# Writing out the counted loops of a four-stage decoder kernel on one core

## The reference, cut to what matters

```python
x = _layernorm(x + _L0_attn_ref(x, ...))           # stage a: grouped attention with rope
x = _layernorm(x + _L0_xattn_ref(x, ctx, itok, ...))  # stage a: latent cross attention
x = _layernorm(x + _L0_ffn_ref(x, ...))            # stage b: 16 experts, 4 chosen, shared expert
x = _layernorm(x + _L1_attn_ref(x, ...))           # stage c: gated delta rule, 32 value heads
x = _layernorm(x + _L1_xattn_ref(x, ctx, mask, ...))  # stage d: 8-bit cross attention
x = _layernorm(x + _L1_ffn_ref(x, ...))            # stage d: top-1 gated attention
```

```python
A  = -(einsum(k_beta, k) * decay) * strict
Tm = solve_triangular(eye - A, eye)
u, kcd = Tm @ v_beta, Tm @ (k_beta * exp(gc))
out = (q * exp(g)) @ St + (q @ k.T * decay) @ (u - kcd @ St)
```

## Time and profile before

| what | value |
|---|---|
| runs (median of 3) | 2425.04 us (2422.2 to 2428.43) |
| the profiled execution, its own time | 2429.71 us |
| its span, first to last instruction | 2428.0 us |
| PE, matmuls, share of the span | 84% |
| DVE, ACT, POOL | 60%, 36%, 6% |
| mean granted PE clock | 0.891 of full |

### The profile page before, as it was taken

How to read it: one execution, slowest core, us unless ns; L and a number is a source line. 1 busy time by engine, 2 the same in 40 slices (tenths; PEclk the granted TensorE clock), 3 DMA queues, 4 the chain that set the end, 5 groups by cost and what they waited for, 6 DMA issues and landing times. The chain is left out here.

```text
span 2428.0 us, 30948 instructions
## 1 busy us (share of the span) xinstructions
PE 2050.6 (84%) x10836; PEld 1521.5 (63%) x10850; DVE 1460.7 (60%) x3251; ACT 880.9 (36%) x1542; POOL 140.1 (6%) x130
## 2 busy tenths in 40 slices
PE   6988987998985889898998989989899883787786
PEld 4867776554553568485684856848668582465454
DVE  3557665323222576767767667676676854657666
ACT  2433433111113445443453534535345431333233
POOL 1011010000002000000000000000000001011110
PEclk8889888999996889999999999999999995787787
DMA  3000000400001120301203012030120202000000
GB/s 125 5 13 9 4 5 24 165 1 9 0 9 56 36 53 19 77 9 36 53 19 79 10 36 53 14 81 11 36 53 14 66 1 68 7 11 9 10 4 5
DMA packets 163244, 78.53 MB, mean 32 GB/s; under 512 B 140530, under 2 KB 152628, under 8 KB 162132
## 3 DMA queue, kind: packets, MB, share of 16 engines
q1 hardware_dynamic: 163124, 76.99, 11.7%
HBM read 59.88 MB, written 16.91 MB: 32 GB/s over the span
## 5 line engine op out<-in xcount | busy, mean ns | idle before, releaser
L1566 DVE TENSOR_TENSOR c_Y<-c_V,c_bank 128x512 f32<-128x512 f32 x192 | 131.9, 687 | 82.2 <-PE c_bank L1239 82.2
L1239 PE MATMUL c_bank<-c_Y,c_NP 128*128 128x128 f32 x1536 | 176.4, 276 | 0.0
L1239 PEld LDWEIGHTS c_bank<-c_Y,c_NP 128*128 128x128 f32 x1536 | 173.9, 192 | 3.3 <-issue 3.3
L1540 DVE SCALAR_TENSOR_TENSOR c_NP<-c_NP,c_cj,c_bank 128x256 f32<-128x256 f32 x256 | 104.9, 476 | 68.5 <-ACT c_NP L1410 68.5
L1172 PE MATMUL c_bank<-c_xT,c_wv 128*128 128x512 f32 x256 | 123.1, 643 | 26.9 <-issue 23.3
L1172 PE MATMUL c_bank<-c_xT,c_wqk 128*128 128x512 f32 x256 | 128.6, 650 | 5.1 <-ACT c_pad L1366 3.1
L1501 DVE SCALAR_TENSOR_TENSOR c_cv<-c_pad,c_wcqk,c_cv 128x1024 f32<-128x1024 f32 x96 | 122.2, 1280 | 12.2 <-ACT c_cv L1380 11.4
L1501 DVE SCALAR_TENSOR_TENSOR c_cv<-c_pad,c_wcv,c_cv 128x1024 f32<-128x1024 f32 x96 | 122.5, 1283 | 4.8 <-ACT c_cv L1380 1.6
L1326 PE MATMUL c_bank<-c_wout,c_yT 128*128 128x256 f32 x512 | 121.3, 383 | 0.0
L1366 ACT ACTIVATE c_pad<-c_bank 128x512 f32<-128x512 f32 x128 | 69.0, 592 | 131.7 <-PE c_bank L1172 131.7
L1172 PEld LDWEIGHTS c_bank<-c_xT,c_wv 128*128 128x128 f32 x256 | 52.2, 207 | 94.4 <-issue 94.1
(11 more groups left out here) (409 smaller groups left out, 4262.3 us busy)
## 6 DMA issues: line engine op xcount, KB each, us to landing
b_wup<-b_in_wup SPq DMA_DIRECT2D x4, 1280.0 KB, 14.3
c_wqk<-c_in_wqk SPq DMA_DIRECT2D x9, 512.0 KB, 3.4
c_wv<-c_in_wv SPq DMA_DIRECT2D x8, 512.0 KB, 3.4
c_wz<-c_in_wz SPq DMA_DIRECT2D x8, 512.0 KB, 5.6
c_wout<-c_in_wout SPq DMA_DIRECT2D x8, 512.0 KB, 4.5
diagonal_blocks<-c_NP SPq DMA_DIRECT2D x64, 64.0 KB
c_A<-diagonal_blocks SPq DMA_DIRECT2D x8, 512.0 KB, 3.5
c_NP<-no_blocks SPq DMA_DIRECT2D x32, 128.0 KB, 3.8
```

What stands on the lines that cost most here:

```text
L1239: last = pe.matmul(banks[n % 4][:, b * P:(b + 1) * P], lhsT(h, 4 * q + b), rhs(h, 4 * q + b), start=True, stop=True)
L1540: dve.scalar_tensor_tensor(NP[:, h, bb, :, :], spread(NP[:, h, bb, 1, :], 2), cj[:, h, bb:bb + 1], gp, ALU.mult, ALU.mult).then_inc(s["NP_ ...
L1566: dve.tensor_tensor(rr(Y, h, q), rr(V, h, q), four(banks[n % 4][:, :]), ALU.subtract).then_inc(s["y_ready"], 1)
```

## The change

Every counted loop of the four stages is written out: `with engine.Fori(a, b) as i:` becomes `for i in range(a, b):`, 18 places, on PE, ACT, DVE, POOL and SP. Work, order, buffers, semaphores and their values stay. What goes is the branches, the register that counts, the register arithmetic in front of waits, and the registers in addresses of DMAs and tiles. What comes is length: each pass now stands in the program.

```diff
@@ stage c, SP
-            with sp.Fori(0, ROUNDS - 1) as i:
+            for i in range(ROUNDS - 1):
                 scatter(i)
                 sp.wait_ge(s["cv_ready"], at(i, CHUNKS, CHUNKS))
                 load_v(i + 1)
@@ stage c, PE, and the same on ACT and DVE
-            with pe.Fori(0, ROUNDS - 1) as i:
+            for i in range(0, ROUNDS - 1):
                 round_(i, True)
             round_(ROUNDS - 1, False)
@@ stage a and stage d, PE, and the same on ACT and DVE
-            with pe.Fori(0, B // LANES - 1) as i:
+            for i in range(0, B // LANES - 1):
                 in_turns([lane_program(i, L, True) for L in lanes])
             in_turns([lane_program(B // LANES - 1, L, False) for L in lanes])
@@ stage b, DVE, and the same on PE, ACT and SP
-            with dve.Fori(0, 2) as i:
+            for i in range(0, 2):
```

More of the change, by code:

```diff
@@ L337, in _ @@
                 sp.sem_inc(L.x2_free, 1)
-            with sp.Fori(0, B // LANES - 1) as i:
+            for i in range(0, B // LANES - 1):
                 for L in lanes:
@@ L373, in _ @@
             pool.sem_inc(consts, 1)
-            with pool.Fori(0, B // LANES) as i:
+            for i in range(0, B // LANES):
                 for c in range(DC):
@@ L574, in _ @@
             in_turns([start_batch(0, L) for L in lanes])
-            with act.Fori(0, B // LANES - 1) as i:
+            for i in range(0, B // LANES - 1):
                 in_turns([lane_program(i, L, True) for L in lanes])
@@ L639, in _ @@
             in_turns([start_batch(0, L) for L in lanes])
-            with dve.Fori(0, B // LANES - 1) as i:
+            for i in range(0, B // LANES - 1):
                 in_turns([lane_program(i, L, True) for L in lanes])
@@ L751, in _ @@
             sp.sem_inc(s["xo_free"], 1)
-            with sp.Fori(0, 2) as i:
+            for i in range(0, 2):
                 sp.wait_ge(s["xo_ready"], at(i, HALF, HALF))
@@ L794, in _ @@
             pe.wait_ge(s["owner_copied"], 16 * (PARTS - 1))
-            with pe.Fori(0, 2) as i:
+            for i in range(0, 2):
                 for t in range(ECH + 2):
@@ L844, in _ @@
                 .then_inc(s["logits_ready"], 1)
-            with act.Fori(0, 2) as i:
+            for i in range(0, 2):
                 act.wait_ge(s["route_step"], at(i, ROUTE, 2))
@@ L1101, in _ @@
             scatter(ROUNDS - 1)
-            with sp.Fori(0, B) as b:
+            for b in range(B):
                 sp.wait_ge(s["xo_ready"], b + 1)
@@ L1131, in round_ @@
                     pool.tensor_tensor(rr(V, h, q), rr(Y, h, q), rr(Y, h, q), ALU.mult).then_inc(s["csq_ready"], 1)
-            with pool.Fori(0, ROUNDS) as i:
+            for i in range(0, ROUNDS):
                 round_(i)
@@ L1465, in _ @@
                 decays(0, n)
-            with act.Fori(0, ROUNDS - 1) as i:
+            for i in range(0, ROUNDS - 1):
                 round_(i, True)
@@ L1615, in _ @@
                 decayed(0, n)
-            with dve.Fori(0, ROUNDS - 1) as i:
+            for i in range(0, ROUNDS - 1):
                 round_(i, True)
```

## The result

The changed kernel takes 2387.93 us (median of 4 runs, 2385.96 to 2391.9), the kernel before 2426.4 us (4 runs, 2422.2 to 2428.43). The ratio is 0.9845, with an interval of [0.9829, 0.9861]. The forecast was 2390. The profiled execution took 2385.96 us and its span is 2383.9 us, 44.1 us shorter than the 2428.0 of the earlier trace rows.

The account below looks back on a forecast made before the run. PE was taken as busiest, held up by missing instructions at stage c's jumps on PE and DVE. 34.9 + 0.8 = 35.7 us off 2429.71 gave 2394.0, less 4.67 for the median 2389.3, rounded 2390; range 2380 to 2396, for all 2378 to 2412.

Parts of the forecast that it names:

- The back edges of stage c: Rounds 1 to 6 without jumps, like the entry into round 7: 146.77 us each, 880.62 against 915.51, 34.9 us gained.
- the holes alone: Time without an instruction to start on DVE at the six back edges of stage c: 20.7 us in all.
- The cover: Stage c: A's gather arrives at 1124.8, before DVE's elimination would want it at 1128.8, leaving 4 us.
- Rival A: Stage c: gain partly hidden because A lands late or DVE waits for ACT; 2407 us, chance 0.12.
- The other stages: Back edges of a, b, d: stage d 0.8 us, stage a nothing with 4 us either way, b nothing to 1 us.
- C: Straight code starves in five former repeat passes of stages a, b and d: 60 us, ending at 2450; chance 0.06.
- D: Register instructions on the path in stages a, b and d: 10 to 20 us more gained, 2375; chance 0.07.
- The rule that spoke against it: Stage c: PE's code memory holds a round, so PE's holes stay and only DVE's go; 8 us gained in all.

Follow-up runs that it names:

- stage c alone: Loops of stage c written out on all engines, those of a, b and d kept, against the kernel before: 2386.99 us, ratio 0.9852.
- SP's stores: The kernel before with only SP's loop of eight stores behind stage c written out: 2427.31 us against 2428.93, one run each.
- DVE alone: The kernel before with only DVE's loop of stage c written out: 2433.26 us, ratio 1.0021.

## Why the prediction was right

**The back edges of stage c.** The sum gave 880.62 us for six rounds, a gain of 34.9; measured 879.98 and 35.53. By pieces, in round 2: from the last addition to the second group of transposes 34.54 forecast, 1152.20 - 1117.65 = 34.55 measured; from there to the first block product 6.32 forecast, 1158.64 - 1152.20 = 6.44 measured; the rest, 105.91 forecast, 1264.26 - 1158.64 = 105.62 measured. The step that carried the forecast was to take round 7 of the kernel before as the picture of a round without a jump. That the holes alone (20.7 us on DVE) undercount was right too, and the kernels with one engine written out show why: PE's hole with the slow clock behind it is the later of the two in most rounds.

**The cover.** The gather of A stayed hidden, as the 4 us in hand said. No DMA stands in front of the first L1552, and all six rounds are alike within 0.34 us. Rival A did not come.

**The other stages.** Stage d gained 0.44 us in this pair of traces (0.8 forecast), and up to the last addition of round 0 the kernels with stages a and b written out took 969.55 to 972.85 us, those with their loops kept 970.04 to 975.92. The two groups overlap, so the 4.69 us of the single pair may be mostly the scatter of one execution; 4.15 of them are already there at the first score of pair 3 of stage a (335.49 against 331.34). More traces show what two could not. In stage a the way from pair 0 to pair 3 took 285.8 to 288.1 us with the loops and 284.6 to 286.7 without. In stage d it took 286.1 to 293.1 us in the nine kernels with its loops and 286.4 to 287.7 in the four without: six of 27 passes with the loops took 98.5 to 98.8 us where the others took 94.9 to 96.0. In two of these kernels the granted clock was read: 0.72 to 0.73 in such passes and 0.77 in the others. No hole stands in them, and whether the loops have a part in it is open. The prediction took the intervals of stage a to be the same whatever code they run; that was read from three intervals and does not hold over all traces, but its bound of 4 us does for this stretch. That stage c alone gives 0.9852 says that the rest is small. Rivals C and D are out.

**A term that was missing.** The text on the change counts 18 loops; the kernel before has 20. SP's loop of eight stores was in the diff and not in the sum: it lies in the 3.35 us from stage c into stage d, of which the kernel with this loop alone showed 2.8. The working counted back edges of the busy engines, and passed over SP because it computes nothing; yet stage d waits for its last issue. With the 3.35 us the sum is 39.05, and the profiled execution took 43.75 less than that of before. The rest, 4.7 us, is the stretch up to round 0. In the medians the gain was 38.5 us. The range of the forecast has a slip: a gain of 31.1 less 4, with 2 us of scatter, ends at 2400 and not at 2396; the result lies inside either.

**The rule that spoke against it.** By the Trainium skill, "Advanced Engine Details and Errata", section ISA Cache, PE's code memory should hold a round, and only DVE's hole should go. The runs show this to be half right. Code stays there: two of six jumps on PE had no hole in the kernel before, none had one with 96 matmuls of padding, and a body of 1,602 instructions returned without a hole. But PE's holes were the jump's all the same, and went with it. A body of 1,802 instructions missed at every back edge, so less can be used for a loop than the page's 128 KB, which at its 256 instructions in 16 KB would by our estimate be 2,048. On DVE it is the same: the section's 32 KB would by the same estimate be 512 instructions and would have held a body of 361, which missed at every back edge; the limit seen lies between 301 and 361. The Trainium skill, "Runtime: NRT & Kernel Launch", section Instruction fetch mechanics, says that a taken branch to a target outside the window stalls until its page is fetched, and that in straight code the fetch is mostly hidden. The trace agrees on both: 2.4 to 4.2 us per missed jump on DVE, 0.34 us from addition to copy without one.

**Where it was right with some luck.** The working took PE's four holes as a property of the kernel. The traces with an unchanged PE program show 4, 5 and 6 holes (the kernel before, SP's stores, DVE alone). Had the profiled execution had none, as with stages a, b and d written out, the same working would have given 25 us (905.68 - 880.62 = 25.1).

**Open.** Why the start of the body is still there at one edge and gone at the next, with the same program, is not settled. PE's body is near the limit (1,638 between 1,602 and 1,802). Two kernels whose loop stands elsewhere had no miss and one had four, so placement probably counts; something that differs between executions or with the other engines' timing decides the rest. Whether this and the longer passes of stage d make the kernel before scatter from 2410 to 2436 us, where the changed one stays within 6, was not tried; it would need traces of many runs.

## What to carry to other kernels

Look for "issue" in the list of waits and at the first instruction behind each back edge: where a loop's body is longer than what the engine keeps (here the limit is between 301 and 361 instructions on DVE and between 1,602 and 1,802 on PE), a pass pays 2.4 to 6.3 us, and where two engines loop together, one alone gives a third of the gain or nothing (here 11.3 and -2.7 of 35.5 us). At a short body's jump no hole was seen (0.17 us on DVE), and the registers cost nothing measurable here; but the loop of an engine that only issues transfers counts where somebody waits for the last of them. A boundary in the kernel that already has no jump, here the one into the last round, priced the change better than the sum of the holes.

## What the runs showed of the hardware that was not expected

- DVE's hole behind a jump does not grow with the body: 2.63 us at 361 instructions, 2.41 at 501, 3.34 with a body of two rounds of stage c.
- A hole on PE went with nine packets of 16.3 KB, more than the six to seven of the whole body: four around the hole, five over the round behind it. In two kernels PE's holes were gone though its loop was not touched, with 384 instructions ahead of it (907.82 us for six rounds against 915.51, but the whole kernel slower, 2455.8 us) and with other stages written out; one trace each.
- With one PE program the number of misses was 4, 5 and 6.
- A DMA issue in SP's loop took 0.82 us, written out 0.47 us.
- Behind a wait of 2.75 us in the middle of a round, eight transposes took 1.97 us at a granted clock of 0.50 and a projection 4.84. With the projection moved into that wait the transposes took 1.04 at 1.00, the projection 3.60 in two rounds and 5.30 in later ones, and six rounds 26.1 us less, three quarters of what the whole change gave there (35.5).
